# ViT tower on one core: norm, turn and logits of the late token tile moved forward in the slot, the two halves of the pixel products put side by side

## The reference, cut to what matters

```python
# tokenizer: x is (32, 256, 64, 64); a token is a patch of 4x4 pixels, 256 tokens an image
q = _ln(reduce_feats, ln_q_w, ln_q_b) @ Wq.T              # from the patch's mean
kv = _ln(unf, ln_kv_w, ln_kv_b) @ Wkv.T                   # from its 16 pixels
attn = softmax(einsum('bhpd,bhpnd->bhpn', q * scale, k))  # 8 heads
h = reduce_feats + (attn @ v) @ proj_w.T + proj_b
h = concatenate([cls_tok, h], axis=1)
# layer: a recurrence over the images (b), for each token position
h = h + scan(h_new = tanh(xp_b + h @ W_hh.T)),  xp = _layernorm(h) @ W_ih.T + biases
# experts: 8, two for each token, routed by a softmax over _layernorm(h) @ router_w.T
h = h + moe(_layernorm(h))
```

## Time and profile before

| | |
|---|---|
| runs | 1656.12 us median, 1655.04 to 1662.23 |
| profiled execution | 1680.15 us, span 1678.3 us |
| mean granted TensorE clock | 0.955 |
| PE busy | 1414.3 us, 84% |
| DVE busy | 1099.1 us, 65% |
| ACT busy | 806.3 us, 48% |
| POOL busy | 708.2 us, 42% |
| DMA | 415.69 MB, mean 248 GB/s |

### The profile page before, as it was taken

How to read it: one execution, slowest core, us unless ns; L and a number is a source line. 1 busy time by engine, 2 the same in 40 slices (tenths; PEclk the granted TensorE clock), 3 DMA queues, 4 the chain that set the end, 5 groups by cost and what they waited for, 6 DMA issues and landing times. The chain is left out here.

```text
span 1678.3 us, 65455 instructions
## 1 busy us (share of the span) xinstructions
PE 1414.3 (84%) x25781; PEld 1083.8 (65%) x25781; DVE 1099.1 (65%) x3070; ACT 806.3 (48%) x2022; POOL 708.2 (42%) x858
## 2 busy tenths in 40 slices
PE   3799999999998989989898989989648888888870
PEld 2577777777777766777676667677536566555550
DVE  3567666766665767866676667777447556776773
ACT  1365565655554655555555556556443333333330
POOL 1233343333333433356655534334147734332536
PEclk9899999999998999999999999999869999999995
DMA  8977787877776876889999786673257646675866
GB/s 285 345 263 279 249 298 259 301 258 272 283 274 241 306 254 237 296 275 316 317 312 324 268 290 257 218 252 133 76 164 229 220 152 182 201 211 172 251 207 178
DMA packets 202089, 415.69 MB, mean 248 GB/s; under 512 B 25952, under 2 KB 126624, under 8 KB 201664
## 3 DMA queue, kind: packets, MB, share of 16 engines
q1 hardware_dynamic: 187504, 372.69, 64.7%
q0 software_dynamic: 14288, 38.82, 7.8%
HBM read 329.52 MB, written 81.89 MB: 245 GB/s over the span
## 5 line engine op out<-in xcount | busy, mean ns | idle before, releaser
L1039 DVE BATCH_NORM_STATS2 st<-xp 128x6 f32<-128x512 f32 x512 | 339.1, 694 | 0.5
L537 POOL TENSOR_TENSOR rs_px<-px_ve,half_neg 128x16 f32<-128x16 f32 x64 | 186.3, 2911 | 296.8 <-DVE px_ve L1044 296.8
L649 ACT ACTIVATE zT<-bank 128x512 f32<-128x512 f32 x256 | 146.2, 598 | 193.0 <-PE bank L872 192.9
L1332 POOL DMA_INDIRECT y<-ys_dram,slot x130 | 125.3, 964 | 188.4 <-DMA ys_dram<-y_s 84.4
L872 PE MATMUL bank<-ident,z_s 128*128 128x128 f32 x1024 | 163.4, 295 | 28.3 <-issue 27.5
L642 ACT ACTIVATE z_s<-bank 128x512 f32<-128x512 f32 x256 | 138.7, 597 | 61.4 <-PE bank L862 61.4
L623 ACT ACTIVATE u<-bank 128x512 f32<-128x512 f32 x256 | 132.2, 603 | 53.6 <-PE bank L812 53.6
L872 PEld LDWEIGHTS bank<-ident,z_s 128*128 128x128 f32 x1024 | 120.8, 149 | 46.9 <-issue 40.2
L832 PE MATMUL bank<-xc,u 128*32 128x64 f32 x8192 | 133.9, 220 | 18.2 <-issue 17.5
L832 PEld LDWEIGHTS bank<-xc,u 128*32 128x32 f32 x8192 | 128.0, 110 | 32.8 <-issue 21.0
L310 POOL DMA_INDIRECT xs_dram<-xrow,slot x130 | 128.4, 988 | 40.3 <-issue 37.5
(11 more groups left out here) (179 smaller groups left out, 3134.6 us busy)
## 6 DMA issues: line engine op xcount, KB each, us to landing
xp<-xpix SPq DMA_DIRECT2D x256, 512.0 KB
xc<-xg SPq DMA_DIRECT2D x256, 512.0 KB
xt<-xs_dram SPq DMA_DIRECT2D x151, 128.0 KB, 3.3
ys_dram<-y_s SPq DMA_DIRECT2D x151, 128.0 KB, 2.6
xs_dram<-zero SPq DMA_DIRECT2D x49, 384.0 KB, 8.2
base_dram<-h SPq DMA_DIRECT2D x65, 128.0 KB, 7.9
rows_dram<-tok SPq DMA_DIRECT2D x65, 128.0 KB, 7.6
hb<-base_dram SPq DMA_DIRECT2D x65, 128.0 KB, 3.0
```

Of the source, the lines that this page charges most:

```text
L537: pool.tensor_tensor(rs_px[:, :], px_ve[:, :], half_neg[:, :], ALU.pow).then_inc(s["px_done"], 1)
L649: act.activation(zT[:, c, :, :].rearrange("p h (a r t) -> p r h a t", r=2, t=TS)[:, r, :, :, :], BIG[f][:, :].rearrange("p (a h t) -> p h ...
L1039: dve.bn_stats(st[:, j, :], xp[u.x][:, 2 * j:2 * j + 2, :].rearrange("p i c -> p c i")).then_inc(s["st_done"], 1)
```

## The change

It moves calls inside the `slot` functions and adds or removes no instruction. On TensorE `turn_tok` goes from behind `project_out` to ahead of `recur`, and `weigh` half 0 goes from ahead of `logits` to behind it (and behind the rank products), next to half 1. On ScalarE `route_turned` goes ahead of `hidden`, and `route_logits` ahead of the first two `z_out`. On VectorE `route_norm` goes from behind `pixel_var` to right behind `token_norm`. GpSimd's and SP's orders stay.

```diff
@@ ScalarE's slot @@
                 if front:
                     u_out(act, u)
+                if late:
+                    route_turned(act, u.k - 4)
                 if end:
                     hidden(act, z)
                 if late:
-                    route_turned(act, u.k - 4)
+                    route_logits(act, u.k - 4)
                 if mid:
                     z_out(act, v, [0, 1])
-                if late:
-                    route_logits(act, u.k - 4)
@@ TensorE's slot @@
                 if mid:
                     turn_p(pe, v)
+                if late:
+                    turn_tok(pe, u.k - 4)
                 if end:
                     recur(pe, z, 0)
                     recur(pe, z, 1)
                 if back:
                     project_out(pe, w)
-                if late:
-                    turn_tok(pe, u.k - 4)
                 if end:
                     turn_h(pe, z)
-                if mid:
-                    weigh(pe, v, front, 0)
                 if late:
                     logits(pe, u.k - 4)
                 for g, part in pieces_now(u.k):
...
                         route_ranks(pe, g, FB)
                 if mid:
+                    weigh(pe, v, front, 0)
                     weigh(pe, v, front, 1)
@@ VectorE's slot @@
                 if end:
                     token_norm(dve, z)
+                if late:
+                    route_norm(dve, u.k - 4)
                 if front:
                     stats(dve, u, [5])
...
                     stats(dve, u, [7])
                     pixel_var(dve, u)
-                if late:
-                    route_norm(dve, u.k - 4)
```

## The result

Over 18 runs of each kernel, taken together, the changed kernel took 1651.92 us (median, 1638.71 to 1662.37) and the kernel before 1664.24 (1653.06 to 1684.54). The ratio is 0.9928, 95% interval 0.9906 to 0.9951: 0.72% faster, about 12 us (8 to 16). The forecast was 0.34%, 5.7 us. The eighteen runs of before lie 8 us above the three on which the forecast stood, so the ratio is what the forecast is to be measured by. The measured gain is twice the forecast one, and its interval leaves the forecast's 5.7 us out.

The account below looks back on a forecast made before the run. TensorE was taken to bound the undisturbed 16.62 us slot. 43 slots at -0.20 us (-8.6), 17 at +0.22 (+3.7) and -0.8 for the rank products gave -5.7 us, 1650.4 us predicted, range 1642 to 1662.

Parts of the forecast that it names:

- Part 1, the halves: TensorE's end of slot: both weigh halves side by side take 1.89 us, so turn_rs starts 0.35 us earlier.
- The rival with the exposed first load: Logits' first load stays exposed behind turn_h, gain 0.22 instead of 0.35 us; also in the slower case, 1669.3 us, chance 0.07.
- rival (a): Larger gain: logits at a pace of 0.11 us, -0.31 us a slot in 43 slots, 1645.7 us; chance 0.25.
- Part 2, the tanh: turn_tok ahead of the recurrence makes ScalarE's tanh late, so turn_h's load starts 0.15 us late (0.12 to 0.32).
- Part 3, q_out: Earlier route_norm on VectorE delays the exponential and q_out, which just fits before project; otherwise up to 0.1 us a slot.
- Part 4, the other loops: Where GpSimd's scatters or VectorE's routing pieces set the slot, later project_out costs 0.22 us: 17 slots, +3.7 us.
- the two slots with the rank products: Rank products waited for the logits' copy on ScalarE; that copy ahead of z_out gives -0.4 us each, -0.8 us.
- rival (d): The same stalls meet a falling granted clock in other slots: +-4.7 us, about 1646 or 1655; chance 0.1.
- The sum: Whole kernel: -8.6 + 3.7 - 0.8 = -5.7 us, 0.34%.
- I leave them where they are: TensorE's issue stalls, placed between the means and the queries' projection, where no TensorE instruction moves, were taken as unchanged.

Follow-up runs that it names:

- the extra change: Changed kernel with turn_rs moved between the two halves, against the kernel before: ratio 0.9915 (0.9878 to 0.9952), undisturbed slot 16.50 us.
- held-back pair: Kernel before and changed kernel, each with the load of xp held back until the next slot's means are through: 1630.74 us (0.9751) and 1624.04 us (0.972).
- turn_tok placed by slot: Changed kernel, tanh ahead of tokT copy, turn_tok behind recurrence, or behind project_out in scatter or routing-piece slots: 0.9973; with xp load held back 0.9679, 1617.15 us.
- logits-last kernel: Kernel before with the logits behind both halves, everything else in its old place: ratio 1.0343; with the load of xp held back 0.9815, 1649.91 us.
- halves alone: Kernel before with only the two halves side by side and the logits' copy ahead of z_out: ratio 1.0105 (1.005 to 1.016), undisturbed slot 16.78 us.
- turn_tok between: Changed kernel with turn_tok between the recurrence and project_out and the tanh ahead of the tokT copy: ratio to the kernel before 0.9956, undisturbed slot 16.27 us.

## Why the prediction was right, and where it was off
**Part 1, the halves: right in kind, too small.** Both in 1.89 us, the logits' first load hidden, no idle time ahead of the halves: 0.35 us less was forecast by the weight loads, and the rows give 2.60 us from turn_h's first load to turn_rs's, against 3.01 before, 0.41. The rival with the exposed first load is refuted by the row of L935, whose loads start at 156.66 while turn_h's products run to 156.94. The logits take 0.44 us, which is the pace of rival (a). Here the Trainium skill's sentence that loads overlap only where the row group differs (TensorE: Matmul & The Clock Gate, Part 3) doesn't hold; the Trainium skill's rule that a change of tiling mode drains the engine (TensorEngine Tiling (Array Packing), Key Properties) agrees, and the extra change gives it a price of 0.16 us.

**Part 2, the tanh: right.** 0.12 us late, where I took 0.15 out of 0.12 to 0.32. Together an undisturbed slot gained 0.28 us where 0.20 was the forecast and 0.31 rival (a). Of the 0.08 us, 0.06 are in the loads and the rest is the tanh. So at the slot it is rival (a), which had 0.25, that nearly came true. One sum in part 1 is wrong: with the first load exposed, 0.13 us a slot in 43 slots bring the forecast 5.6 us nearer to no change, and not 2.5.

**Part 3, q_out: right.** The exponential came 0.32 us later, q_out started at 8.54 instead of 8.41 and ended at 9.15; project started at 9.31 as before. It fitted by 0.16 us.

**Part 4, the other loops: right in kind and in the size of a slot, wrong in the count and at the rank products.** In the held-back pair, slot against slot, the thirteen slots 39 to 51 cost 0.22 us each where neither a stall nor the clock disturbs them, and so do slots 32 to 34, 37, 56 to 58 and 61 with routing pieces, 0.16 to 0.22: 21 slots, where the forecast had 17. Among the 21 are the two slots with the rank products, which were to be 0.4 us shorter. They are 0.22 and 0.16 us longer (18.98 to 19.20, 18.78 to 18.94): the wait for the logits' copy fell from 0.78 to 0.27, but the means of the next slot now wait 0.45 us for the copy of the ranks. Slots 38 to 51 lost 5.1 us in all, where 9 x 0.22 = 2.0 was forecast. Thirteen slots at 0.22 are 2.9; four falls of the clock add about 6, and fewer stalls take the rest back. The forecast had no term for the clock behind a longer wait; its rival (d) let the clock fall by stalls alone. The kernel with turn_tok placed by slot takes the loss in the slots with scatters away.

**The sum.** With all measured terms it reads 39 x -0.28 + 21 x 0.21 = -6.5 us. The forecast's -5.7 is near it because its errors cancel: 0.08 us too little a gaining slot is 3.4 us on one side, and four gaining slots that pay, with the rank products, are about 2.6 us on the other. That is luck, and 6.5 us is also only about half of the measured 12 us (8 to 16), whose interval leaves it out. The rest isn't explained by the order. In both pairs of profiles the changed kernel has less issue idle in slots 5 to 62, 37.5 against 50.8 us and 53.7 against 58.5, but two profiles of one kernel differ by as much. What stays is that each part of the slot is shown, and that the total came out in the range partly by stalls and clock that the forecast held constant.

**The weakest step** is the one sentence on the stalls, "I leave them where they are". The load of xp keeps its place 0.1 us ahead of the slot in this change, but the stalls are not fixed: in slots 4 to 37 the logits-last kernel has 50.8 us of issue idle where the kernel before has 27.6 and 21.6 in its two profiles, and holding the load back takes away half to two thirds of the issue idle of slots 5 to 62, which is worth about three times the change. They don't all lie between the means and the queries either: three, 1.8 us in all, stand at the recurrence (L911), where the change does move instructions. Five of the ratios that I forecast from undisturbed slots (halves alone, turn_tok between, logits last, the extra change of tiles, placed by slot) lie outside the measured intervals, though four of their slots came out within 0.05 us. The orders with the shortest slots (turn_tok between recurrence and project_out, and placed by slot) came out at 0.9956 and 0.9973 without the hold-back, with the load in its usual place; why their stalls take back what their slots give isn't settled. Each profile is one execution, and two of the same kernel before differ by 17.5 us in slots 4 to 37.

That the place of SP's loads sets much of the issue idle is shown by what moving them does. That TensorE waits for its instructions in these stalls is inferred from the packet of the instruction queue that starts 2.2 to 2.5 us before the end of each long one. Where the packet waits, in the queue's order or in the engines' share, no run here tells. The hold-back also moves the stores and the load of xc behind it, by SP's order, and these weren't tried apart, so it may be either load. Open too is why slots 38 to 51 of the kernel before took 284.6 us in the profile of the second group and 259.4 in the first profile: in slot 42 the copy of the means on ScalarE started 3.7 to 5.8 us into the slot in every kernel of the first two groups, and 2.00 in the first profiles.

## What to carry to other kernels
Read the price of an order from the weight loads, not from the products, and look for a stretch of the same trace that already has the new order: slot 3 gave the 1.89 us. Then ask which slots are set by another loop, and whether the step moved lies in that loop; a step can be free in one place in 39 slots and cost in the other 21, and code written out by hand may place it by slot. A wait that grows by tenths where another loop sets the slot can cost microseconds if the clock falls behind it, so read the granted clock slot by slot. And before an order is tuned by tenths, see whether "issue" stalls of microseconds recur in the engine with the most instructions, and try to move the large loads away from them.

## What the runs showed of the hardware that I had not expected
Starting the 2 MB load of xp 2.0 us into a slot instead of 0.1 us before it, with the stores and the load of xc behind it, made the kernel before 2.5% faster in one group, and gave the changed one 0.972 against 0.9928 and 0.9912 in others; in the changed one TensorE's issue idle, all its rows added, was 12.8 us instead of 37.5 and 53.7 in 58 slots. The packets of the instruction queue have 16 KB (3.51 MB in 214), and in the kernel before one starts 2.2 to 2.5 us before the end of each stall over 1.3 us. A change between tiles of 64 x 32 and the whole array costs 0.16 us. On the whole array a following product's weights load while the one before runs, at a pace of 0.11 us, even for products of 8 columns. Behind waits of 1.26 to 1.64 us for another engine and 0.47 for a second one, the granted clock fell to 1.2 GHz for 3.4 us in five slots of 58, at about 1.6 us each; waits as long in other slots left it as it was.
